# A decoder layer on one core: the attention output projection in pairs of sequences and three products of parts, cut into halves, with a reordered norm and a new end

## The reference

```python
q = (x @ wq).reshape(b, n, H, DH).transpose(0, 2, 1, 3)
k = (ctx @ wk).reshape(b, j, H, DH).transpose(0, 2, 1, 3)
v = (ctx @ wv).reshape(b, j, H, DH).transpose(0, 2, 1, 3)
sim = jnp.einsum("bhid,bhjd->bhij", q, k) * SCALE      # masked
attn = jax.nn.softmax(sim, axis=-1)
out = jnp.einsum("bhij,bhjd->bhid", attn, v)
out = out.transpose(0, 2, 1, 3).reshape(b, n, INNER)   # INNER = 1024
return out @ wo + bo                                   # the output projection
...
x = layernorm(x + attention(x, x, ...), ln1_g, ln1_b)
x = layernorm(x + attention(x, enc_output, ...), ln2_g, ln2_b)
```

## Time and profile before

| | |
|---|---|
| runs | 501.25, 499.67, 500.81 us; median 500.81 |
| profiled execution: its own time | 499.44 us |
| its span, first to last instruction | 497.6 us |
| granted TensorE clock, mean | 0.995 |
| busy share: TensorE, VectorE, ScalarE, GpSimd | 95%, 77%, 74%, 52% |

### The profile page before, as it was taken

How to read it: one execution, slowest core, us unless ns; L and a number is a source line. 1 busy time by engine, 2 the same in 40 slices (tenths; PEclk the granted TensorE clock), 3 DMA queues, 4 the chain that set the end, 5 groups by cost and what they waited for, 6 DMA issues and landing times.

```text
span 497.6 us, 14153 instructions
## 1 busy us (share of the span) xinstructions
PE 471.0 (95%) x4668; PEld 433.1 (87%) x4668; DVE 384.3 (77%) x1847; ACT 366.9 (74%) x1390; POOL 257.2 (52%) x355
## 2 busy tenths in 40 slices
PE   8778999999999999999999999999999999999892
PEld 7768889999998999999999999999999997798671
DVE  3678778888988877887787777777777777538875
ACT  4647888778677788877778887777777778836763
POOL 3656356676566555555545444445544555633432
PEclk9999999999999999999999999999999999999997
DMA  8750000000000005000000000000000000400003
GB/s 229 238 207 1 1 3 1 2 2 2 1 3 1 2 4 125 1 3 1 3 1 2 2 2 2 3 2 3 1 1 3 1 2 4 168 1 1 6 7 96
DMA packets 15720, 14.18 MB, mean 28 GB/s; under 512 B 2848, under 2 KB 13344, under 8 KB 15520
## 3 DMA queue, kind: packets, MB, share of 16 engines
q1 hardware_dynamic: 14080, 12.81, 8.3%
q10 hardware_dynamic: 1568, 0.47, 0.4%
HBM read 12.10 MB, written 1.18 MB: 27 GB/s over the span
## 4 chain that ended last, share of the span: by engine, by line
PE 70%; DVE 15%; ACT 5%; issue 4%; DMA 2%; POOL 2%; SPq 1%; POOLq 0%; DVEq 0%; ACTq 0%
PE late_bank L592 11%; PE late_bank L544 10%; PE late_bank L561 10%; PE late_bank L576 10%; PE late_bank L72 8%; PE late_bank L74 8%; PE late_bank L73 8%; ACT P L839 3%; DVE P L1104 3%; DVE ffstats L1260 2%; PE late_bank L601 1%; DMA x<-in_xT 1%; PE late_bank L621 1%; PE late_bank L622 1%; PE late_bank L623 1%
## 5 line engine op out<-in xcount | busy, mean ns | idle before, releaser
L839 ACT ACTIVATE P<-P,at_negmax 128x128 f32<-128x128 f32 x512 | 199.0, 397 | 79.1 <-DVE at_negmax L1104 79.1
L1535 POOL TENSOR_TENSOR P<-P,at_inv 128x512 f32<-128x512 f32 x128 | 136.6, 1079 | 122.3 <-DVE at_inv L1114 122.2
L1130 DVE COPY at_PT<-late_bank 128x512 f32<-128x512 f32 x128 | 87.7, 688 | 35.4 <-PE late_bank L544 35.4
L1104 DVE CUSTOM_DVE_ANT_0 P<-late_bank,maskb 128x128 f32<-128x128 f32 x512 | 110.4, 286 | 2.4 <-PE late_bank L561 2.4
L839 ACT ACTIVATION_READ_ACCUMULATOR P<-P,at_negmax 128x1 f32 x512 | 100.3, 196 | 0.0
L544 PE MATMUL late_bank<-ident,P 128*128 128x128 f32 x512 | 76.4, 273 | 2.0 <-DVE at_negmax L1104 1.0
L544 PEld LDWEIGHTS late_bank<-ident,P 128*128 128x128 f32 x512 | 59.8, 140 | 8.5 <-issue 4.0
L561 PE MATMUL late_bank<-at_k,at_q 64*128 64x128 f32 x1024 | 65.8, 278 | 0.9 <-DVE at_k L1122 0.9
L561 PEld LDWEIGHTS late_bank<-at_k,at_q 64*128 64x128 f32 x1024 | 59.7, 188 | 4.8 <-issue 1.2
L576 PE MATMUL late_bank<-at_PT,V 128*64 128x128 f32 x1024 | 63.0, 276 | 0.0
L576 PEld LDWEIGHTS late_bank<-at_PT,V 128*64 128x64 f32 x1024 | 55.2, 137 | 3.9
(11 more groups left out here) (197 smaller groups left out, 1062.3 us busy)
## 6 DMA issues: line engine op xcount, KB each, us to landing
ctxT_raw<-in_ctxT SPq DMA_DIRECT2D x1, 1024.0 KB, 8.7
out<-xres SPq DMA_DIRECT2D x4, 224.0 KB, 2.6
x<-in_xT SPq DMA_DIRECT2D x1, 768.0 KB, 11.0
xres<-in_x SPq DMA_DIRECT2D x1, 768.0 KB, 14.9
tap_rows<-in_short_wT SPq DMA_DIRECT2D x3, 192.0 KB, 5.0
sa_wq_raw<-in_sa_wq SPq DMA_DIRECT2D x1, 512.0 KB, 6.9
sa_wk_raw<-in_sa_wk SPq DMA_DIRECT2D x1, 512.0 KB, 9.6
sa_wv_raw<-in_sa_wv SPq DMA_DIRECT2D x1, 512.0 KB, 11.2
```

The lines of the kernel that those rows point to most:

```text
L839: last = nc.scalar.activation(P[:, n % 2, h, :], P[:, n % 2, h, :], ACT.Exp, scale=-1.0, bias=negmax[:, n % 2, h:h + 1], accum_out=total[: ...
L1104: last = nc.vector.tensor_tensor_reduce(P[:, n % 2, h, :], score_bank(h), k.maskb[:, cols(n)], scale=1.0, scalar=3.0e38, op0=ALU.add, op1= ...
L1130: nc.vector.tensor_copy(PT[:, HQ * g:HQ * g + HQ, :], banks[T_BANK[g % 2]][:].rearrange("p (h l) -> p h l", h=HQ)).then_inc(pt_ok, 1)
L1535: nc.gpsimd.tensor_tensor(tile, tile, inv[:, n % 2, HQ * g:HQ * g + HQ].unsqueeze(2).to_broadcast([128, HQ, 128]), ALU.mult).then_inc(norm ...
```

## The change

**The product.** `out_proj` works on a pair of items. The weight is the stationary operand and `OT` of both sequences the moving one (256 columns), and it is a split product: `wo` and `OT` are cut in high and low parts. A pair takes eight chunks by three products. The first four chunks (half 0) are issued at the end of odd periods (`FIRST_HALF`, item pair (p-3)/2), the other four (half 1) in even periods behind `transposes(p-1, 0)` (`SECOND_HALF`, pair (p-4)/2). The result is transposed, so ScalarE copies it out (`out_turned`) and TensorE turns it back (`turn_back`, two transposes) in the same even period.

**The parts of OT.** For chunks 0 to 3 ScalarE's copy writes the high part and VectorE's new `ot_low` the low part, from PSUM; for chunks 4 to 7 ScalarE writes a raw copy and GpSimd's new `split_ot` makes both parts with a copy and a subtraction. `wo` is split once for each attention (`out_high` on ScalarE, `out_low` on GpSimd).

**The norm in pairs.** `residual`, the moments (now `statistics`, a step of its own and late in VectorE's even period), `inverse_deviation`, `normalise`, `affine`, `next_residual`, `x_transpose`, `xT_high` and `xT_low` treat two sequences at once: residual and moments in even periods, normalise to `xT_low` in the odd period behind (`NORM`, pair (p-5)/2). The transposes of `X` stand behind the second values half.

**Moved.** `x1_low` goes behind the last `pt_out`, `x1_transposes` behind `transposes(p-1, 2)`, the weights of cross-attention from periods 1 to 6 to periods 3 to 8; `ctxT` and `wo_ca` are loaded later, into memory that other tiles leave. The end's lists are new.

```diff
+        FIRST_HALF, SECOND_HALF, NORM = -3, -4, -5
...
+            def out_proj(t, half):
+
+                if t is None:
+                    return
+                pe.wait_ge((ot_lo, ot_split)[half], 2 * t + 2)
+                if half == 0:
+                    wait(pe, xT_lo, t)
+                    wait(pe, r_ok, t)
+                    wait(pe, x1lo, before(t + 4))
+                    pe.wait_ge(wo_lo, att_pair(t) + 1)
+                w = out_w[att_pair(t)]
+                for c in range(4 * half, 4 * half + 4):
+                    for wo, ot in ((w.hi, OT.hi), (w.hi, OT.lo), (w.lo, OT.hi)):
+                        last = nc.tensor.matmul(banks[W_BANK][:, 0:PCOLS], wo[:, c, :], ot[:, c, :],
+                                                start=(c == 0 and wo is w.hi and ot is OT.hi),
+                                                stop=(c == H // 2 - 1 and wo is w.lo))
...
+            def turn_back(t):
+
+                if t is None:
+                    return
+                pe.wait_ge(outT_ok, t + 1)
+                for b in range(PAIR):
+                    last = nc.tensor.transpose(turned_back()[:, b], outT[:, b * 128:(b + 1) * 128], k.ident[:])
+                last.then_inc(back_mm, 1)
...
 
             for p in range(ITEMS):
-                x_transpose(p - 4)
                 v_half(p, 0)
                 unit(p, 0)
                 transposes(p - 1, 0)
+                out_proj(item_pair(p, SECOND_HALF), 1)
                 unit(p, 1)
                 v_half(p, 1)
+                x_transpose(item_pair(p, NORM))
                 transposes(p - 1, 1)
+                turn_back(item_pair(p, SECOND_HALF))
                 unit(p, 2)
-                x1_transposes(p, transposed_in(p))
+                if p == 1:
+                    x1_transposes(p, transposed_in(p))
                 if p == 0:
                     mixer_output(p, 2)
                 transposes(p - 1, 2)
+                if p != 1:
+                    x1_transposes(p, transposed_in(p))
                 projection(p, pair_of(p, PROJECT), 0)
                 projection(p, pair_of(p, PROJECT - 1), 2)
                 unit(p, 3)
                 transposes(p - 1, 3)
                 projection(p, pair_of(p, PROJECT), 1)
                 mixer_output(p, pair_of(p, OUTPUT))
-                out_proj(p - 2)
+                out_proj(item_pair(p, FIRST_HALF), 0)
                 scores(p + 1)
                 p_v(p - 1)
 
-            x_transpose(ITEMS - 4)
+            out_proj(PAIRS - 2, 1)
             transposes(ITEMS - 1, 0)
             transposes(ITEMS - 1, 1)
             pe.wait_ge(k.ff_lo, 1)
@@ -786,22 +843,22 @@
             wait_result(0)
             hidden(k, pe, 0, (0, 1))
             second_bias(0)
+            turn_back(PAIRS - 2)
...
-            out_proj(ITEMS - 2)
+            hidden(k, pe, 0, (2, 3))
             p_v(ITEMS - 1)
-            x_transpose(ITEMS - 3)
-            hidden(k, pe, 0, (2, 3))
-            out_proj(ITEMS - 1)
+            x_transpose(PAIRS - 2)
             wait_result(1)
-            hidden(k, pe, 1, (0, 1))
-            x_transpose(ITEMS - 2)
+            hidden(k, pe, 1)
+            out_proj(PAIRS - 1, 0)
+            out_proj(PAIRS - 1, 1)
             fc2_sum(k, pe, 0)
-            x_transpose(ITEMS - 1)
-            hidden(k, pe, 1, (2, 3))
+            turn_back(PAIRS - 1)
             wait_result(2)
             hidden(k, pe, 2, (0, 1))
             next_fc2(1)
+            x_transpose(PAIRS - 1)
             hidden(k, pe, 2, (2, 3))
             wait_result(3)
             hidden(k, pe, 3, (0, 1))
...
-                wait(act, o_mm, n - 1)
-                nc.scalar.activation(OT[:, n % 2, 4 * o:4 * o + 4, :],
+                wait(act, o_mm, 2 * (n // PAIR - 1) + o + 1)
+                tile, done = ((OT.hi, ot_hi), (OT_raw, ot_ok))[o]
+                nc.scalar.activation(tile[:, 4 * o:4 * o + 4, n % 2 * 128:(n % 2 + 1) * 128],
                                      banks[O_BANK[o]][:].rearrange("p (c l) -> p c l", c=4),
...
+            def ot_low(n):
+
...
+                vec.wait_ge(ot_hi, n + 1)
+                part = np.s_[:, 0:4, n % 2 * 128:(n % 2 + 1) * 128]
+                nc.vector.tensor_tensor(OT.lo[part], banks[O_BANK[0]][:].rearrange("p (c l) -> p c l", c=4),
+                                        f32(OT.hi[part]), ALU.subtract).then_inc(ot_lo, 1)
...
                 mixer_shift(2 if p == 1 else pair_of(p - 1, OUTPUT))
-                normalise(p - 3)
+                normalise(item_pair(p, NORM))
                 reciprocals(p, 0)
                 reciprocals(p, 1)
-                xT_low(p - 4)
                 pt_out(p - 1, 0)
+                ot_low(p - 2)
                 k_out(p, 1)
                 pt_out(p - 1, 1)
+                residual(item_pair(p, SECOND_HALF))
+                xT_low(item_pair(p, NORM))
                 pt_out(p - 1, 2)
-                x1_low(transposed_in(p))
                 k_out(p, 3)
                 pt_out(p - 1, 3)
+                x1_low(transposed_in(p))
+                statistics(item_pair(p, SECOND_HALF))
                 inner_convolution(pair_of(p, CONVOLVE))
                 mixer_residual(pair_of(p, OUTPUT))
                 mixer_statistics(pair_of(p, OUTPUT))
                 reciprocals(p, 2)
                 if p % 2:
...
                 elif p in (12, 13):
                     context_low(p - 12)
                 elif p == NSEQ:
                     feed_forward_low()
                 elif p == NSEQ + 2:
                     bias_low()
-                residual(p - 2)
                 reciprocals(p, 3)
                 maxima(p + 1, 0)
                 maxima(p + 1, 1)
 
-            normalise(ITEMS - 2)
-            xT_low(ITEMS - 3)
-            residual(ITEMS - 1)
-            xT_low(ITEMS - 2)
-            normalise(ITEMS - 1)
+            ot_low(ITEMS - 1)
+            normalise(PAIRS - 2)
+            xT_low(PAIRS - 2)
+            residual(PAIRS - 1)
+            statistics(PAIRS - 1)
             residual_sum(0)
+            normalise(PAIRS - 1)
             residual_moments(0)
-            xT_low(ITEMS - 1)
+            xT_low(PAIRS - 1)
             gained(0)
             outer_sums(0)
...
+            def split_ot(n):
+
...
+                pool.wait_ge(ot_ok, n + 1)
+                part = np.s_[:, 4:8, n % 2 * 128:(n % 2 + 1) * 128]
+                nc.gpsimd.tensor_copy(OT.hi[part], OT_raw[part]).then_inc(ot_part, 1)
+                pool.wait_ge(ot_part, n + 1)
+                nc.gpsimd.tensor_tensor(OT.lo[part], OT_raw[part], f32(OT.hi[part]), ALU.subtract).then_inc(ot_split, 1)
...
                     mixer_residuals(pair_of(p, TRANSPOSE - 1))
-                affine(p - 3)
-                next_residual(p - 3)
-                for g in range(QUARTERS):
-                    normalise(p, g)
+                affine(item_pair(p, NORM))
+                normalise(p, 0)
+                normalise(p, 1)
+                split_ot(p - 2)
+                next_residual(item_pair(p, NORM))
+                normalise(p, 2)
+                inverse_deviation(item_pair(p, SECOND_HALF))
```

283 lines of the change are left out of this document (167 added, 116 removed).

## The result

The changed kernel takes **522.19 us** (median of four runs, 519.5 to 523.95) against 500.94 for the kernel before: a ratio of 1.043, 95% interval 1.039 to 1.047. Forecast was 515.5, in a range of 506 to 522. The direction was right; the time lies 6.7 us above the forecast and just outside the range.

What follows compares the result with a forecast made beforehand. Bounds: TensorE in plain periods, TensorE and VectorE nearly tied in the mixer's even ones, VectorE in the end. Terms -2.1 + 8.7 - 1 - 1.5 + 11.3 = +15.4 on 499.44 gave 514.8; forecast 515.5, range 506 to 522.

Steps and rivals of the forecast that it cites:

- TensorE's work, 0.62 less a pair: Projection on TensorE: a pair of periods falls from 23.92 to 23.30 us if nothing waits.
- The stall at `at_k`: Plain even periods: the scores wait 0.55 us for the copy of keys, which the old projection had covered.
- Plain periods, -1: Ten pairs behind the mixer: each gains 0.1 us after the new stall, -1 us in all, between -6 and +4.
- the splits of `wo` and the rest of periods 11 to 17 lie beside other work: 0: Splits of `wo` and the remainder of periods 11 to 17: run beside other work and cost 0.
- VectorE's moments make that at most 1.7: Plain periods: maxima begin at most 1.7 us behind the scores' start, up from 1.2, and don't suffer.
- Rival D: X waits in plain periods too if GpSimd's split lands on the normalise: +5 to +10, 521 to 525 us; chance 0.10.
- The lock rule: Shared SBUF ports: whichever of such a VectorE and a GpSimd instruction starts first blocks the other; the sum had nothing for it.
- Even mixer periods, +2.9 each, less 2.1: Periods 4, 6, 8: VectorE's later tail and late X cost +2.9 us each, +8.7; period 2 gives -2.1.
- The last period, -1.5: Scores of item 30 to 31: loses the projection, 1.88 us less, with 0.4 more stall: -1.5 us.
- The end, +11.3: Behind the last scores: `ffR` at 36.5 instead of 28.7 us, first gain at 42.3 instead of 31.0: +11.3.
- rival C: Loop as forecast, end half as late since the four groups catch up in VectorE's idle time: 510.5 us; chance 0.10.
- Rivals A and B: A: TensorE alone decides, 492 us, chance 0.06; B: the loop gains, only the end loses, some 502, chance 0.09.

Runs made afterwards that it cites:

- fill_stalls: Changed kernel with products of no use placed where TensorE stands idle, at three mixer waits and one in the end: 521.05 us.
- lists_anew: Changed kernel, same instructions, with the lists of four engines in another order in mixer, plain periods and end: 496.06 us.
- probe_plain: Changed kernel with two products of no use ahead of the scores in every period from 12 on: 525.06 us.
- x_low_moved: Changed kernel with affine ahead of the mixer's residuals, X transposed behind the second transposes of probabilities, cross-attention's low weights in periods 9 to 11: 512.01 us.
- half_left_out: Changed kernel with 9 of 12 products left out of the projection's second half for pairs 0, 1 and 2: 516.92 us.
- x_first: Changed kernel with GpSimd making X of a pair (affine) ahead of the mixer's residuals of the same odd period: 519.13 us.
- end_back: Changed kernel with only its end's VectorE and TensorE lists put nearer to the old order: 516.36 us.

## Why the prediction was right and wrong

The direction was right and the time was not: 522.19 us against 515.5. The full-clock profile (fill_stalls) is the one to hold against the sum of +15.4. It has +18.3 of span: 515.9 against 497.6. So 2.9 of the 6.7 us that are missing are errors of the sum. The other 3.8 lie between an execution at full clock and the median: 4.5 us, where the forecast had added 0.7. Two steps failed: the plain periods, in which VectorE's late work was put at nothing, and the clock, which had no term.

- **TensorE's work, 0.62 less a pair: right in kind, 0.1 to 0.2 too much.** By the starts in the trace the two halves take 1.60 and 1.51 us, 3.11 against 3.76, with the crossings of fp32r and transposes; the sum had 2.88 and one crossing of 0.08. In all, the projection's 60.2 us (32 x 1.88) became 49.8 (16 x 3.11). By the busy time that the forecast named as its sign, 62.5 us fell to 53.4 and not to some 45. Where nothing waits a pair takes 23.41 (lists_anew), forecast 23.30.
- **The stall at `at_k`: right.** 0.44 us measured, 0.55 forecast, in each even plain period; probe_plain shows that it is idle time.

```profile
316.14 0.60 PE L581 MATMUL late_bank<-ident,P 128*128 128x128 f32 x4
317.18 2.06 PE L598 MATMUL late_bank<-at_k,at_q 64*128 64x128 f32 x32 [0.44 <-DVE at_k L1196]
```

- **Plain periods, -1: wrong, this step failed.** The ordinary pairs take 23.95 us, not 23.85: no gain. And "the splits of `wo` and the rest of periods 11 to 17 lie beside other work: 0" does not hold, nor does "VectorE's moments make that at most 1.7" for the start of the maxima behind the scores. The pairs from items 12, 16 and 18 take 1.06, 0.35 and 1.18 us more than before. In the even periods 12, 16 and 18 VectorE makes low parts (of the context, of the feed-forward weights, of the biases). Before, `ctxT_lo` of period 12 was made ahead of item 13's scores (at 205.12), and the maxima began 1.3 us behind them:

```profile
204.29 1.20 DVE L1252 TENSOR_TENSOR ctxT_lo<-ctxT_raw,ctxT_hi 128x1024 fp32r<-128x1024 f32 x1
...
206.43 0.26 DVE L1104 CUSTOM_DVE_ANT_0 P<-late_bank,maskb 128x128 f32<-128x128 f32 x1
```

Now no projection stands between the last unit and the scores (at 218.84), and the low part stands behind the moments and ahead of the maxima, which begin 2.5 us behind them:

```profile
220.17 1.19 DVE L1346 TENSOR_TENSOR ctxT_lo<-ctxT_raw,ctxT_hi 128x1024 fp32r<-128x1024 f32 x1
...
221.37 0.26 DVE L1178 CUSTOM_DVE_ANT_0 P<-late_bank,maskb 128x128 f32<-128x128 f32 x1
```

In period 21, with no low part ahead of it, they begin at 1.4; in 17 and 19 at 2.0 and 2.7. The transposes of probabilities then start 0.7, 0.2 and 0.9 us later in periods 13, 17 and 19 than in 21. This is read from the timelines; no run took the low parts away. The transposes of X wait 0.25 us more in each of the three, and x_low_moved, where X is transposed later, took just that off, so X's part is shown. Together the plain periods have +2.9 where the sum had -1: 3.9 us, the largest miss. Rival D had X late in plain periods; it is, but for 0.25 us in three of them and not for 5 to 10 us in all. Nor is D's mechanism seen. The 32 subtractions of `split_ot` took 1.27 to 1.30 us and the copies 0.60 to 0.63, and just one of them ran beside a VectorE instruction that reads SBUF alone. The lock rule that the forecast quoted from the Trainium skill (SBUF — State Buffer, "SBUF: two separate sides") has next to nothing to work on there. Where such meetings are, they are as before: beside `ctxT_lo` a multiplication of GpSimd took 1.93 us in both kernels, where most take 1.04. The subtraction itself was priced at 1.04 and took 1.29, which nothing waited for.
- **Even mixer periods, +2.9 each, less 2.1: right.** At full clock the pairs of intervals from items 4 and 6 are 2.7 longer (30.84 against 28.18), the pair from item 8 3.4, and period 2 is 2.0 shorter. The two causes hold: half 1 ahead of the last unit goes in one to one (half_left_out), X is late by 0.9, not 1.2 (x_first). The third pair's 3.4 is 0.5 above the forecast. The stretch is +7.1, forecast +6.6.
- **The last period, -1.5: measured -1.2.**
- **The end, +11.3: the path right, the sum 2 too high.** `ffR` came 36.4 us behind the last scores (forecast 36.5), the gain at 42.0 (42.3), for the reasons given (end_back). But behind the gain the rest took 46.0 instead of 47.6 (before: 78.6 - 31.0), all of it behind the fourth gain. The kernel catches up there, a small part of rival C. Which order of which engine is worth how much of the lateness was not parted.
- **The clock: no term, and it needed one; this step failed too.** The full-clock execution took 517.69 us, the median 522.19. By the profiles that were taken, falls of the clock cost 0.4 each in the loop, 1.3 in the start and nothing to 4.3 in the end; that they make up the 4.5 us between is an estimate from these. The forecast had seen a clock of 0.91 in the last stretch of before and did not ask what new waits of TensorE would do to it. Which of these falls an execution has differs from one to the next; why, these runs don't tell.

One execution at 517.69, inside the range, is the ground for saying that the sum alone would have held; the medians of the changed kernel (522.19, 521.29) lie on both sides of the range's edge. That the errors of the sum nearly cancel is luck in part: 3.9 too little in the plain periods stand against 2.0 too much in the end. Rivals A and B are out: the plain periods did not come at 11.6 throughout, and the loop lost. C is out with the gain at 42.

## What to carry to other kernels

When work leaves a busy engine, look at what it covered: 1.88 us of products stood between a unit and the scores. Without them the copy of keys, done 1.0 us behind the unit, came into view, and VectorE's low parts, which had been made in that time, came to stand ahead of the maxima. Cover is spent only once, so a list of one engine that was laid out against the old work has to be laid out again: the order alone took the changed kernel from 522 to 496 us and the kernel before from 500 to 496, while the new arithmetic is worth 4 to 5 in the loop and the end with a last pair is 5.8 longer. And a new wait on TensorE is priced twice, by its length and by the half clock that may follow: 0 to 0.4 us a fall where TensorE has to wait behind it anyway, 1.3 where it does not, and up to 4.3 for the several falls of the end.

## What the runs showed that I had not expected

- A subtraction on GpSimd of 512 columns that writes fp32r takes 1.29 us, where a multiplication of the same size that writes float32 takes 1.04; the copy to fp32r takes 0.61. Whether the operation or the type makes the difference was not tested.

```profile
L1649 POOL TENSOR_TENSOR at_OT_lo<-at_OT_raw,at_OT_hi 128x512 fp32r<-128x512 f32 x32 | 41.3, 1290 | 2.6
...
L1647 POOL CAST at_OT_hi<-at_OT_raw 128x512 fp32r<-128x512 f32 x32 | 19.6, 612 | 21.0 <-ACT at_OT_raw L924 21.0
```

- The granted clock fell behind stretches in which TensorE had been busy for 2.42 and 2.10 of 4 us, and it did so in one execution of a program but not in the next. The same end took 87.9 to 92.3 us.
- Another order of the lists did not shorten the plain periods of the kernel before at all (11.95 against 11.95): there the busy share of TensorE, 59.80 of 59.80 us, had said everything.
